# Queries stored row by row and turned by the transfer that loads them, not by TensorE

## The reference

```python
q = jnp.einsum('bsd,ed->bse', x, Wq).reshape(bsz, seqlen, HQ, D)   # 32 heads of 128
k = jnp.einsum('bsd,ed->bse', x, Wk).reshape(bsz, seqlen, HK, D)   # 8 heads
q = _rope(_rmsnorm(q, q_norm_w), pos)
k = _rope(_rmsnorm(k, k_norm_w), pos)
...
scores = jnp.einsum('bqhd,bkhd->bhqk', q, k_all) * SCALE           # 512 cached + 32 new keys
probs = jax.nn.softmax(jnp.where(valid, scores, -1e+30), axis=-1)
o = jnp.einsum('bhqk,bkhd->bqhd', probs, v_all)
x = x + jnp.einsum('bse,de->bsd', o.reshape(bsz, seqlen, HQ * D), Wo)
```

## Time and profile before

| | |
|---|---|
| median of 3 runs | 2153.13 us (2148.91 to 2156.41) |
| the profiled execution | 2149.25 us, of which the span of the trace is 2147.5 |
| TensorE busy | 2073.0 us, 97% |
| VectorE busy | 1684.0 us, 78% |
| ScalarE busy | 1477.6 us, 69% |
| GpSimd busy | 1103.8 us, 51% |
| granted TensorE clock, mean | 0.987 |
| moved by DMA | 510.05 MB, 238 GB/s |

### The profile page before, as it was taken

The page is one execution under the profiler, slowest core; times in us unless marked ns, Lnnn a source line. Parts: engine busy times, 40 slices in busy tenths (PEclk is TensorE's granted clock), DMA queues, the critical chain, the costliest instruction groups (busy, mean ns, idle before and its releaser), DMA issues.

```text
span 2147.5 us, 55920 instructions
## 1 busy us (share of the span) xinstructions
PE 2073.0 (97%) x17337; PEld 1358.1 (63%) x17337; DVE 1684.0 (78%) x4299; ACT 1477.6 (69%) x4204; POOL 1103.8 (51%) x1854
## 2 busy tenths in 40 slices
PE   6898999999999978999999999999999999999999
PEld 3444555555555556677777777777777777777775
DVE  7787888888877777777777777787777777777774
ACT  2575777777776766667777777777777777777774
POOL 4464656565655544545454545445454545454542
PEclk9999999999999989999999999999999999999999
DMA  9655777665666589988888888888888888888881
GB/s 352 201 187 165 228 228 235 222 223 191 202 221 220 201 268 303 288 262 247 245 255 248 254 250 257 239 257 246 257 246 251 251 252 248 249 256 248 245 247 55
DMA packets 399642, 510.05 MB, mean 238 GB/s; under 512 B 50931, under 2 KB 297587, under 8 KB 396788
## 3 DMA queue, kind: packets, MB, share of 16 engines
q1 hardware_dynamic: 361972, 371.71, 55.7%
q0 software_dynamic: 37376, 134.76, 19.5%
HBM read 413.77 MB, written 92.54 MB: 236 GB/s over the span
## 4 chain that ended last, share of the span: by engine, by line
PE 58%; SPq 1%; DMA 1%; DVE 1%; issue 1%; DVEq 0%; ACT 0%; POOL 0%; POOLq 0%
PE att_y L1679 15%; PE att_scores L1629 14%; PE att_tr L1638 10%; PE att_o L1665 5%; PE att_o L1666 5%; PE att_o L1667 5%; PE att_tr_new L1644 1%; PE att_o L1668 1%; PE att_scores L1630 1%; SPq L126 1%; DMA att_keys<-k_parts 1%; SPq L120 0%; DVE att_prob L1782 0%; DVE att_tpl L1806 0%; SPq L117 0%
## 5 line engine op out<-in xcount | busy, mean ns | idle before, releaser
L1782 DVE CUSTOM_DVE_ANT_0 att_prob<-att_scores,att_mask 128x544 f32<-128x544 f32 x512 | 371.0, 725 | 293.6 <-PE att_scores L1630 249.3
L1708 ACT ACTIVATE att_tph<-att_tr 128x512 f16<-128x512 f32 x512 | 306.3, 598 | 329.6 <-PE att_tr L1638 319.5
L1578 POOL CAST att_parts<-att_norm 128x96 f16<-128x96 f32 x512 | 135.9, 265 | 562.1 <-issue 551.7
L1679 PE MATMUL att_y<-att_wo,att_ot 128*128 128x512 f16 x1536 | 408.2, 379 | 0.0
L1806 DVE TENSOR_TENSOR att_tpl<-att_tr,att_tph 128x512 f16<-128x512 f32 x512 | 350.3, 684 | 0.7 <-ACT att_tph L1708 0.6
L1638 PE MATMUL att_tr<-ident,att_norm 128*128 128x128 f32 x2048 | 326.8, 282 | 0.0
L1229 POOL TENSOR_TENSOR proj_rn<-proj_ra,proj_rb 128x512 f32<-128x512 f32 x128 | 190.4, 1488 | 211.9 <-DVE proj_rb L1342 211.9
L1665 PE MATMUL att_o<-att_tph,att_values 128*128 128x128 f16 x1536 | 284.0, 219 | 2.9 <-ACT att_of L1708 1.9
L1666 PE MATMUL att_o<-att_tpl,att_values 128*128 128x128 f16 x1536 | 283.9, 219 | 0.0
L1667 PE MATMUL att_o<-att_tph,att_values 128*128 128x128 f16 x1536 | 283.8, 219 | 0.0
L1140 ACT ACTIVATE proj_square<-proj_blk 128x128 bf16<-128x128 f32 x640 | 168.8, 281 | 127.4 <-PE proj_blk L1098 127.3
(11 more groups left out here) (233 smaller groups left out, 5345.5 us busy)
## 6 DMA issues: line engine op xcount, KB each, us to landing
room<-k_parts SPq DMA_DIRECT2D x512, 128.0 KB, 2.3
att_keys<-k_parts SPq DMA_DIRECT2D x512, 128.0 KB
q_parts<-proj_turned SPq DMA_DIRECT2D x128, 256.0 KB, 3.6
v_new_parts<-proj_vp SPq DMA_DIRECT2D x64, 256.0 KB, 3.1
room<-q_parts SPq DMA_DIRECT2D x32, 512.0 KB, 6.8
att_query<-q_parts SPq DMA_DIRECT2D x32, 512.0 KB
w<-in_w_t SPq DMA_DIRECT2D x12, 1024.0 KB, 20.9
room<-in_k_t SPq DMA_DIRECT2D x8, 1024.0 KB, 6.7
```

What stands on the lines that cost most here:

```text
L1679: last = mm(y_ps[:, :], ot[p][:, a, h, :], wo[:, h, w, :], start=(h == 0 and start), stop=(h == HQ - 1 and stop))
L1708: copy = lambda out, in_, **kw: nc.scalar.activation(out, in_, ACT.Copy, **kw)
L1782: v.tensor_tensor_reduce(out=prob[q][:, :], in0=sc[q], in1=mask[bi % 2][:, at:at + LK], scale=1.0, scalar=-3.0e38, op0=ALU.add, op1=ALU.ma ...
```

## The change

Queries are no longer turned by TensorE. ScalarE and VectorE split the rotated block `rn` where it lies, in SBUF, with rows on the partitions; the store writes 128 rows of 1024 f16 (512 high, 512 low) into `q_parts`, now of the shape (2048 rows, 8192). The load of a sample reads its 32 rows of 8192 and turns them on the way (`transpose=True`), so that it leaves the same layout in `query` as before. Keys are turned by TensorE as before, with the semaphore `tq_done` now counting keys alone. The add on GpSimd into a buffer of `rn` waits for the low half of the block that lay there (`low`), where it waited for its turn.

```diff
@@ load_sample
-    sp.dma_start(query[:, :, :, :].rearrange("p h two c -> p h (two c)"),
-                 q_d[ds(t, 1), :, :, bi, :].rearrange("o g p c -> p (o g) c")).then_inc(loaded, 16)
+
+    sp.dma_start(query[:, :, :, :].rearrange("p g two (h s) -> p (g two h) s", s=S), q_d[ds(b * S, S), :],
+                 transpose=True).then_inc(loaded, 16)
@@ conditional_residual
-    q_d = nc.dram_tensor("q_parts", (NT, QB, P, BT, 2 * HB * S), F16).ap()
+    q_d = nc.dram_tensor("q_parts", (B * S, QB * 2 * D), F16).ap()
@@ head_views
             if n < QB:
-
-                src = tq[n % 2][:, :].rearrange("p (h b s) -> p b h s", h=HB, b=BT)
-                dst = buf[:, :].rearrange("p (b two h s) -> p b two h s", b=BT, two=2, h=HB)
-                return src, dst[:, :, 0], dst[:, :, 1]
+                return rn[n % NR][:, :], buf[:, 0:D], buf[:, D:2 * D]
@@ store_heads
                 if n < QB:
-                    dst = q_d[ds(t, 1), n].rearrange("o p b c -> (o p) b c")
-                    src = src.rearrange("p (b c) -> p b c", b=BT)
+                    dst = q_d[ds(t * P, P), n * 2 * D:(n + 1) * 2 * D]
@@ tensor: turn_heads becomes turn_keys
-                if n < QB:
-                    pe.wait_ge(sum_done, idx + 1)
-                    src = rn[n % NR]
-                else:
-                    pe.wait_ge(kn_done, t * KB + n - QB + 1)
-                    src = kr[n - QB]
-                after(pe, high, idx - 1)
-                after(pe, low, idx - 1)
+                pe.wait_ge(kn_done, t * KB + n - QB + 1)
+                after(pe, high, (t - 1) * ROT + n + 1)
+                after(pe, low, (t - 1) * ROT + n + 1)
+                src = kr[n - QB]
@@ tensor: body
-                    if heads_at(t, n):
-                        turn_heads(*heads_at(t, n))
+                    if heads_at(t, n) and heads_at(t, n)[1] >= QB:
+                        turn_keys(*heads_at(t, n))
@@ scalar: heads_high
-                idx = t * ROT + n
-                act.wait_ge(tq_done, idx + 1)
+                if n < QB:
+                    act.wait_ge(sum_done, t * ROT + n + 1)
+                else:
+                    act.wait_ge(tq_done, t * KB + n - QB + 1)
@@ gpsimd: add
                 if n >= QB:
-                    after(pool, tq_done, (t - 1) * ROT + n + 1)
+                    after(pool, tq_done, (t - 1) * KB + n - QB + 1)
                     out = kr[n - QB]
-                elif n >= NR:
-                    pool.wait_ge(tq_done, t * ROT + n - NR + 1)
-                    out = rn[n % NR]
                 else:
-                    after(pool, tq_done, (t - 1) * ROT + n + QB - NR + 1)
+                    after(pool, low, t * ROT + n - NR + 1 if n >= NR else (t - 1) * ROT + n + QB - NR + 1)
                     out = rn[n % NR]
```

More of the change, by code:

```diff
@@ L1064, in turn_x, with turn_keys @@
                 last.then_inc(xturned, 1)
-            def turn_heads(t, n):
-                idx = t * ROT + n
-                if n < QB:
-                    pe.wait_ge(sum_done, idx + 1)
-                    src = rn[n % NR]
-                else:
-                    pe.wait_ge(kn_done, t * KB + n - QB + 1)
-                    src = kr[n - QB]
-                after(pe, high, idx - 1)
-                after(pe, low, idx - 1)
+            def turn_keys(t, n):
+                pe.wait_ge(kn_done, t * KB + n - QB + 1)
+                after(pe, high, (t - 1) * ROT + n + 1)
+                after(pe, low, (t - 1) * ROT + n + 1)
+                src = kr[n - QB]
                 for h in range(HB):
@@ L1114, in _ @@
             for n in range(QB, ROT):
-                turn_heads(NT - 1, n)
+                turn_keys(NT - 1, n)
         @block.scalar
```

## The result

The changed kernel takes 2275.6 us (median of 5 runs, 2259.3 to 2317.6) against 2151.3 before: 1.055 times as long, 95% interval 1.052 to 1.058. The forecast was 2254, slower, with a range from 2108 to 2430.

What follows compares the result with a forecast made beforehand. TensorE was taken to bound projections and attention. To the execution of 2149.25 us came 9 for VectorE becoming the projections' bound and 92 for the turning load: 2250, with 3.9 for the median 2254; range 2108 to 2430.

Steps and rivals of the forecast that it cites:

- The lock: Projections: VectorE instructions with two SBUF inputs and GpSimd's SBUF reads exclude each other; 5.6 us more per tile, net +9.
- the late pages: Attention: pages queued behind the turning transfer on SyncE land late and TensorE waits for keys; 92 us.
- The turns on TensorE: Projections: 8 of 10 turns per tile go, 3.5 us per tile, 56 us over 16 tiles if nothing else fills up.
- VectorE's need: Projections: VectorE's work per tile before the change, 35.9 less 5.0 us of waits, 30.9; after it 36.5.
- VectorE without idle time: Projections: sign of the blocking, together with low halves lasting about 0.7 and about 1.9 us.
- The load that turns: Attention: one 512 KB transfer per sample, issued second in the load, delays all queued behind it; 92 us.
- X: Attention: extra time of the turning load over the plain one, taken as 2.4 us, between 1.2 and 5.1.
- 22.4: Attention: predicted period of a sample in us, instead of 21.0.
- the spare 1.0 us: Attention: a normal load lands 20.0 us into a 21.0 us sample, so only delay beyond 1.0 us costs time.
- Rival 2: The turning load fits and VectorE is not held up in the projections: the 56 us go, 2097; chance 0.24.
- Rival 1: The turning load fits in the 1.0 us spare in attention, VectorE still fills up: 2162; chance 0.19.
- Rival 3: The turn in attention is much dearer, 5.1 us or more: 2424 and up, over 4500 if broken into elements; chance 0.17.

Runs made afterwards that it cites:

- e3: e1 with the first input of the queries' low half on VectorE read from a PSUM tile instead of SBUF; 2103.5 us, ratio 0.979.
- e1: The changed kernel with a plain load of the queries again, same 512 KB per sample; 2174.9 us, ratio 1.011.
- e2: The kernel before with only the load of the queries changed to the turning transfer; 2256.5 us, ratio 1.047.
- e4: The kernel before with the plain load of the queries cut into 8 transfers of 64 KB on the same queue; 2259.8 us, ratio 1.051.
- e6: The changed kernel with the row scales of a sample loaded by one transfer instead of four; 2216.3 us, ratio 1.033.
- e5: The kernel before with the plain load of the queries in two transfers, 2048 pieces of 256 bytes; 2211.1 us, ratio 1.030.
- e7: The changed kernel with the turning load issued by ScalarE on its own queue in 8 transfers of 64 KB; 2349.9 us, ratio 1.096.
- e8: e7 with TensorE copying the high half of each query block into PSUM, where VectorE subtracts it; 2328.3 us, ratio 1.083.
- e9: The changed kernel with a third query buffer, the turning load issued one sample ahead and last in the load; 2229.1 us, ratio 1.037.
- e11: e9 with the row scales of a sample in one transfer instead of four, the lock left in; 2175.4 us, ratio 1.011.
- e10: e9 with one row-scale transfer and TensorE copying the queries' high halves into PSUM for VectorE's low half; 2150.1 us, ratio 0.999.
- e12: e10 with the copy of a tile's last query block moved behind the next tile's first block; 2136.7 us, ratio 0.993.

## Why the prediction was right

It forecast 2254 where 2275.6 was measured (+101 against +124), by two steps. The lock held in its mechanism; the late pages held too, but what makes them late was priced from the wrong quantity, and that the price came near is partly luck.

**The turns on TensorE** are worth what was said: e3, where nothing fills up, is 47 us under the kernel before, of 56. **The lock** is as drawn from the rows: e3 shows it, and the pattern is the one predicted, 1.76 us behind a chunk's low half, 1.38 behind a reduction of Wo, 0.67 behind a rotation. The size is off: +24 us (e1) for +9 (16 x 0.6 is 9.6, which should have been +10). The mis-sized term is VectorE's need, "35.9 - 5.0 = 30.9". I took its whole idle time as usable. Of 5.0 us per tile 2.7 stayed idle in the changed kernel (its row of waits for the squares has 26.7 us and that for the copies 7.8 in the same 480, now 12.7 tiles), since TensorE stops for up to 4.8 us for VectorE's copy of the next x, starts again at a granted clock of 0.50, and VectorE then waits for TensorE's first blocks. The sign that the prediction named, "VectorE without idle time", did not come for the same reason.

**The load that turns**: +92 forecast, 106 measured (e2). The price X = 2.4 us was a middle between bounds of engine time, and the engines' time did rise by 3.0 us in e2 (61.4% of 16 x 2265.6 us against the earlier trace rows, over 64 samples). But e4 moves the pages without any engine time, and e6 has 2.7 us of it with 0.5 us of waits for keys. What moved them is SyncE, which issues the turning transfer for a median of 4.1 us instead of 0.43 and the row scales for 2.0 instead of 2.5: the last page came 3.1 us later. That an engine time of 2.4 and an issue of 3.1 are of like size is luck. The sixteen pages themselves went out as before once they had started (9.03 us in e4, 9.62 in the earlier trace rows).

Per load the forecast was close: the period rose by 1.40 us in e2's profiled execution, and 22.4 was said for 22.54. The shortfall lies in the first eight loads, in which SyncE also loads the pieces of Wo: 34.5 us longer in e2, where the sum has 4 x 2.4 + 4 x 1.4 = 15. Above a delay of about 1 us the periods grow, as the spare 1.0 us said, though by less than one for one: e5 is 2.3 us late and loses 0.6 per load, e4 3.0 and 1.7. And TensorE waited for keys in 20 of some 58 loads of the changed kernel from 860 to 2200 us, not in each.

**What the prediction did not have** are the waits for the values. It named what is queued behind the turning transfer on SyncE; these are loads of GpSimd's queue. They appear in every run with the turning transfer and the four row-scale transfers on SyncE's queue, not in those with plain queries (e4, e5) or with the turn on ScalarE's queue (e7, e8), stay when the turning load is moved to the end (e9), and go when the four become one there (e11, e10, e12). In e6, with one row-scale transfer but the turning load ahead of the pages, 27.2 us stay. By which way the small transfers and the turning one hold up the indirect loads is open; no run measured it by itself.

**The rivals.** Rival 2 needed no lock: it exists (e3, 2103) only where the second input is not in SBUF. Rival 1 needed a load that fits: that is e11 with 2175, where rival 1 said 2162. Rival 3 did not come; the transfer is not broken into elements. By an estimate from the 261 GB/s of the Trainium skill (DMA: Bandwidth & Descriptors, "Latency and other measured facts") the load would have cost 0.3 us more on the engines; it cost 3.0 in e2 and 0.9 in e11. By an estimate from the 1309 ns per block of the Trainium skill (VectorE: DVE Perf Modes, "The three transpose paths") it would be 21 us for a sample; the one landing that the changed kernel's trace gives for it is 9.0 us after the issue. The measurements decide against 21, and against 0.3 where other loads are in the way.

## What to carry to other kernels

Before an operand is moved from PSUM to SBUF on VectorE, look in the timeline for GpSimd instructions that start when the one ahead of it ends: a 0.68 us subtraction became 1.76 where an add of GpSimd was already waiting. Price a transfer by how long it holds the queue that issues it and what is queued behind it, not by its bytes alone; if it must be dear, put it last, with a buffer more, so that nothing of the current step waits for it. And idle time of the next engine is not all room: with a hand-over once per tile half of it stayed idle here.

## What the runs showed of the hardware beyond that

A turning transfer of 512 KB moves in 2048 packets of 256 bytes. It holds SyncE for 2.6 to 12.5 us in the changed kernel (median about 4), and for a median of 2.3 in e11, where it is issued last and the row scales are one transfer; one of 64 KB holds ScalarE for 1.3 us (e7), so eight of them cost 10. The same 512 KB plain in 256-byte pieces cost the engines 1.1 us more than in 512-byte pieces (57.4% of 16 x 2208.1 us against the earlier trace rows, over 64 samples), turned 3.0 us more in e2 and 0.9 in e11. And four transfers of 1 KB per sample, which nobody would count, decided 54 us between e9 and e11.
